# Four-layer graph network on one core: the first layer's scatters add to three DRAM tables in turn instead of four

## The chip, the cores and the metric

The kernel runs on one core of one Trainium2 chip (a core is a set of engines: TensorE, written PE; VectorE, DVE; ScalarE, ACT; GpSimd, POOL; SyncE, SP; with 16 DMA engines beside them). The metric is the device time of one execution in microseconds, as the median over repeated runs; lower is better.

## What is computed

Four message-passing layers run one behind the other on 3125 nodes with 160 features and 100,000 edges. Each layer normalises the nodes, applies a ReLU, builds a message of each edge and adds the messages up by node. The change lies in the first layer, whose reference, cut to what matters, is this:

```python
w = relu(edge_feature @ W_fc1) @ W_fc2            # 224 weights an edge
src, dst = edge_index
xs, xv = s[dst], v[dst]
tp = concatenate([out0a, out0b, out1a, out1b, out1c])   # 480 numbers an edge, from w, xs, xv, edge_attr
agg = segment_sum(tp, src, num_segments=N) / 32.0
out_s = agg[:, :96] @ W_out_s + skip_s
out_v = einsum('nmi,mk->nki', agg[:, 96:].reshape(N, 128, 3), W_out_v) + skip_v
```

The edges are sorted by `dst`. This layer gathers by `dst` and sums by `src`, so its sums go to scattered rows. The other three layers sum by `dst` and keep their sums on the core.

## The kernel before

The edges are padded to 832 tiles of 128 (ALL_TILES), four tiles to a group (GROUP), 208 groups (ALL_GROUPS). The program is written out by hand for each engine and has no planner: each engine's block is a list of instructions in order, and semaphores join the blocks. A barrier of all five engines stands between stages. In the first layer the stages are: the setup, the preparation of the nodes, the edge loop, and the loop behind it (`post`), which works on 25 slots of 128 nodes.

**The setup.** SP loads the inputs and writes zeros over each table `src_sum[c]` (line 420, one DMA of 6240 KB per table). Then it writes the keys (line 425) and comes to the barrier. DVE meanwhile works out the index tables and scales the weights (lines 1361 to 1479).

**The edge loop.** For a group, SP loads the keys (line 474, 256 KB) and the edge features (line 460, 128 KB). PE makes the weights and picks the rows by `dst`, and DVE makes the messages (lines 1574 to 1622 and the many multiplications, which all carry line 1332, that of a helper). In `sums` PE multiplies each tile's 128 messages by a 0/1 matrix (line 1072), so that edges of one tile with the same `src` share one sum. ACT copies each product of 128 x 480 from PSUM to the buffer `E.run` (`run_out`, line 812), which holds two groups. POOL then adds those 128 rows to rows of a table in DRAM (`scatter`, line 628: an indirect DMA with an add, one for each tile, 832 in all). Two such scatters may hit the same row. Those that add to the same table must therefore follow one another: each waits until the last one on its table has landed (semaphore `put[c]`). With CHAINS = 4 tables, tile t of each group goes to table t. ACT waits, before it writes over a piece of `E.run`, until the scatter of two groups earlier that read it has landed.

**The loop behind it.** For each slot SP loads 128 rows of each table (240 KB each, line 511) into `Nv.car`, with two buffers. DVE adds the pieces (`sums`, the lines of 128x480), PE transposes the sum (line 984) and multiplies it by the output weights (lines 1091 and 1093), ACT copies the transposes (lines 850 and 851), and DVE copies the product out (line 1745). On DVE the copy of slot j-2 stands ahead of the additions of slot j; on PE the transposes of slot j stand ahead of the products of slot j-1.

Of the kernel before, what the change touches and what calls it, by code (L numbers as in the profile page):

```python
# [20 lines left out]
ALU = mybir.AluOpType  # L21
# [13 lines left out]
GROUP = 4  # L35
# [5 lines left out]
ALL_TILES = TILES + 2 * MORE  # L41
ALL_GROUPS = ALL_TILES // GROUP
PAD_NODE = ROWS - 1
S, V = 64, 32
CHAINS = 4
DEPTH = 4
ZERO_AT = 18432 - 480

# [53 lines left out]
def build(nc, a, out, layers=(0, 1, 2, 3)):  # L102
    with ExitStack() as ctx:
        def sb(name, shape, dt=F32):
            return ctx.enter_context(nc.sbuf_tensor(name, shape, dt))
# [4 lines left out]
        def dram(name, shape, dt=F32):  # L110
            return nc.dram_tensor(name, shape, dt, kind="Internal").ap()
# [4 lines left out]
        dst_table = dram("dst_table", (ROWS, DIM))  # L116
        src_sum = [dram(f"src_sum{c}", (TABLE_ROWS, SPEC[0]["f"])) for c in range(CHAINS)]
        edge_h = dram("edge_h", (TILES * P, DIM))
# [18 lines left out]
        put_i = sb("put_i", [P, ALL_TILES], I32)  # L137
# [70 lines left out]
        dve_own, act_own, pool_own = sem("dve_own"), sem("act_own"), sem("pool_own")  # L208
# [28 lines left out]
        keys_in = [sem(f"keys_in{b}") for b in range(DEPTH)]  # L237
        put = [sem(f"put{c}") for c in range(CHAINS)]
        s = type("Signals", (), one)
# [52 lines left out]
        def node_views():  # L292
            g = carve()
            v = type("Node", (), {})
            v.h = g(2, DIM)
            v.hT = g(2, 4, P)
            v.big = g(SLOTS * DIM)
            v.small = g(8, SLOTS)
            v.smi = g(SLOTS, dt=I32)
            v.rden = g(SLOTS, 4)  # L300
            v.car = g(2, 4 * 480)
            v.sum = g(2, 480)
            return v

        Nv = node_views()

        def l3_views():
# [90 lines left out]
        def _(sp):  # L398
# [105 lines left out]
            def post():  # L504
                def stage(j, b, first, half):
                    if not first:

                        sp.wait_ge(s.sum_free, 1)
                        sp.sem_inc(s.sum_free, -1)
                    for c in range(CHAINS):  # L510
                        sp.dma_start(Nv.car[:, b, c * 480:(c + 1) * 480],
# [69 lines left out]
        @block.gpsimd  # L581
        def _(pool):
            own = Steps()
            last_row = pool.to_reg(ROWS - 1)
            last_table_row = pool.to_reg(TABLE_ROWS - 1)

            def gather(dst, table, idx, bound):
                return pool.indirect_dma_start(dst, None, table, bass.IndirectOffsetOnAxis(ap=idx, axis=0),  # L588
                                               bounds_check=bound, oob_is_err=True)


            nc.gpsimd.memset(U.zero, 0.0).then_inc(pool_own, own.step())
            nc.gpsimd.memset(ident[:], 0.0).then_inc(pool_own, own.step())
            nc.gpsimd.memset(lower[:], 1.0).then_inc(pool_own, own.step())
            nc.gpsimd.iota(U.columnI, pattern=[[1, P]], base=0, channel_multiplier=0).then_inc(pool_own, own.step())
            nc.gpsimd.iota(U.trashI, pattern=[[0, 2]], base=ROWS, channel_multiplier=1).then_inc(pool_own, own.step())
            pool.wait_ge(pool_own, own.n)
            nc.gpsimd.affine_select(out=ident[:], in_=ident[:], compare_op=ALU.not_equal, fill=1.0, base=0,
                                        pattern=[[-1, P]], channel_multiplier=1).then_inc(pool_own, own.step())

            nc.gpsimd.affine_select(out=lower[:], in_=lower[:], compare_op=ALU.is_gt, fill=0.0, base=0,
                                        pattern=[[-1, P]], channel_multiplier=1).then_inc(pool_own, own.step())
            pool.wait_ge(pool_own, own.n)
            pool.sem_inc(pool_own, own.reset())
            pool.sem_inc(zero_made, 2)

            barrier(pool, "pool")

            def gathers_by_src(l):
                def stage(g):  # L610
                    if g >= DEPTH:

                        pool.wait_ge(s.messages_done, (l - 1) * ALL_GROUPS + g - DEPTH + 1)
                    for t in range(GROUP):
                        e = g * GROUP + t
                        gather(W.got[:, g % DEPTH, t, :], node_table[l], src_i[:, e:e + 1], last_row).then_inc(
                            got[l][g % DEPTH], 16)
                return stage

            def scatter(g):  # L620
                for t in range(GROUP):
                    e = g * GROUP + t

                    if g:
                        pool.wait_ge(put[t], g * 16)

                    pool.wait_ge(s.run_out, e + 1)
                    pool.indirect_dma_start(  # L628
                        src_sum[t], bass.IndirectOffsetOnAxis(ap=put_i[:, e:e + 1], axis=0),
                        E.run[:, g % 2, t * 480:(t + 1) * 480], None, compute_op=ALU.add,  # L630
                        bounds_check=last_table_row, oob_is_err=True).then_inc(put[t], 16)

            barrier(pool, "pool")

            pool.wait_ge(zeroed, 16 * CHAINS)
            unrolled(ALL_GROUPS, [(0, scatter)])
            barrier(pool, "pool")
            barrier(pool, "pool")
            for l in (1, 2):
                nc.gpsimd.memset(acc_view(l), 0.0).then_inc(s.acc_zeroed, 1)  # L640
                barrier(pool, "pool")
                unrolled(ALL_GROUPS, [(0, gathers_by_src(l))])
                barrier(pool, "pool")
                barrier(pool, "pool")
            if 3 in layers:
                barrier(pool, "pool")

                def gather_both(g):
                    b = g % DEPTH
                    if g >= DEPTH:  # L650

                        pool.wait_ge(s.rows_added, g - DEPTH + 1)
                    for t in range(GROUP):
                        e = g * GROUP + t
                        gather(T.gs[:, b, t, :], src_table, src_i[:, e:e + 1], last_row).then_inc(
                            got[3][b], 16)
                        gather(T.gd[:, b, t, :], dst_table, dst_i[:, e:e + 1], last_row).then_inc(
                            got[3][b], 16)
                unrolled(GROUPS, [(0, gather_both)])
                barrier(pool, "pool")  # L660
                barrier(pool, "pool")
                nc.gpsimd.memset(acc_view(3), 0.0).then_inc(s.acc_zeroed, 1)
                barrier(pool, "pool")
                barrier(pool, "pool")
# [13 lines left out]
        def _(act):  # L678
# [17 lines left out]
            for name, key in (("fc2_1", "L1_gnn_fcW2"), ("fc2_2", "L2_gnn_Wfc2"), ("rbf", "L3_gnn_W_rbf")):  # L696
                for to, at, n in BY_Y0:
                    n = min(n, wt[name].shape[1] - to)
# [104 lines left out]
            def run_out(g):  # L803
                b, f = g % 2, SPEC[0]["f"]
                for t in range(GROUP):
                    n = g * GROUP + t
                    if g >= 2:

                        act.wait_ge(put[t], (g - 1) * 16)

                    act.wait_ge(s.run_mm, n + 1)
                    act.activation(E.run[:, b, t * f:(t + 1) * f], bank[:, 6 + n % 2, 0:f], ACT.Copy).then_inc(s.run_out, 1)  # L812
# [78 lines left out]
            prep(0)  # L891
            barrier(act, "act")
            unrolled(ALL_GROUPS, [(0, run_out), (-2, fc_out), (-3, relu_out)])
            for t in range(GROUP):
                act.wait_ge(put[t], ALL_GROUPS * 16)
            barrier(act, "act")
            post()
            barrier(act, "act")
# [428 lines left out]
        def _(dve):  # L1327
            V_ = nc.vector
            c = Steps()

            def tt(o, p, q, op):
                return V_.tensor_tensor(o, p, q, op)  # L1332
# [388 lines left out]
            def post(l):  # L1721
# [3 lines left out]
                def sums(j, b, first, half):  # L1725
                    f = SPEC[0]["f"]

                    dve.wait_ge(s.carry_in0 if b == 0 else s.carry_in1, 16 * CHAINS)
                    dve.sem_inc(s.carry_in0 if b == 0 else s.carry_in1, -(16 * CHAINS))
                    car = Nv.car[:, b, :]  # L1730
                    o = Nv.sum[:, b, 0:f]
                    tt(o, car[:, 0:f], car[:, f:2 * f], ALU.add).then_inc(dve_own, c.step())
                    tt(car[:, 2 * f:3 * f], car[:, 2 * f:3 * f], car[:, 3 * f:4 * f], ALU.add).then_inc(dve_own, c.step())
                    dve.wait_ge(dve_own, c.n)
                    tt(o, o, car[:, 2 * f:3 * f], ALU.add).then_inc(dve_own, c.step())
                    dve.wait_ge(dve_own, c.n)
                    dve.sem_inc(dve_own, c.reset())
                    dve.sem_inc(s.sum_ready, 1)
                    dve.sem_inc(s.sum_free, 1)
# [452 lines left out]
```

## Time and profile before

| what | us |
|---|---|
| median of 3 runs | 8548.7 (8541.74 to 8609.48) |
| the profiled execution's own time | 8655.61 |
| its span | 8653.9 |
| in it: setup and preparation, up to the first edge work | about 205 |
| the edge loop of the first layer | about 205 to 1954 |
| the loop over 25 slots behind it | about 1954 to 2100 |
| layers two to four | the rest |

The profile is of one execution. Starts and durations in it are in microseconds from the span's start. "Busy" is the time in which an engine executes. An idle time is given with what ended it. The granted clock is TensorE's, as a share of full speed. The share of DMA is the mean busy share of the 16 DMA engines, in which a packet counts for the whole of its time, and two that overlap count twice, so that it can pass 1.

### The profile page before, as it was taken

To read this page: it belongs to the slowest core of one execution; us is meant where nothing else is said; L and a number is where in the kernel's file an instruction comes from. 1 tells how busy PE (TensorE), PEld (TensorE's weight loads), DVE (VectorE), ACT (ScalarE), POOL (GpSimd) and SP (SyncE) were. 2 spreads that over 40 slices of the span, in tenths; PEclk is the share of its full clock that TensorE was granted. 3 is DMA by queue.
4 is the path that set the end of the run, shared out by engine and by line. 5 is a ranking of instruction groups with operands and counts; after the bars stand their busy time and mean duration, and the time that the engine had idled before them with its cause. 6 is when DMAs were issued, how large, how long until landed. Compare 5 with 4: busy or idle time off the path is not lost. (4 is left out here: it accounts for less than half of the span.)

```text
span 8653.9 us, 111370 instructions
## 1 busy us (share of the span) xinstructions
PE 7204.2 (83%) x32226; PEld 4840.7 (56%) x32226; DVE 6840.9 (79%) x20357; ACT 3363.3 (39%) x8451; POOL 4980.2 (58%) x4078
## 2 busy tenths in 40 slices
PE   3999999993899999699999947788888888886567
PEld 1444444443455455445544537677777777775455
DVE  5999999994677777577777748778887878787895
ACT  1444444441333233323332325455555555554000
POOL 0777777770566666267766517667767667662000
PEclk9999999995799999689999958888998988898796
DMA  4999999993122222022222112222222222221342
GB/s 163 162 165 169 168 166 168 167 156 117 54 56 57 55 57 56 24 57 61 60 58 59 51 33 67 71 72 75 77 77 72 75 74 75 73 71 47 107 140 80
DMA packets 459615, 776.94 MB, mean 90 GB/s; under 512 B 96641, under 2 KB 310886, under 8 KB 458758
## 3 DMA queue, kind: packets, MB, share of 16 engines
q0 software_dynamic: 274944, 469.50, 28.0%
q1 hardware_dynamic: 178166, 299.52, 11.0%
q8 instruction: 269, 4.41, 0.2%
q14 instruction: 332, 2.72, 0.1%
q10 hardware_dynamic: 5904, 0.79, 0.1%
HBM read 464.60 MB, written 304.85 MB: 89 GB/s over the span
## 5 line engine op out<-in xcount | busy, mean ns | idle before, releaser
L588 POOL DMA_INDIRECT fore<-node_table,src_i x1664 | 1766.6, 1062 | 961.2 <-issue 494.8
L1332 DVE TENSOR_TENSOR work<-work 128x384 f32<-128x384 f32 (+4 forms) x4726 | 1784.7, 406 | 198.5 <-ACT work L922 91.4
L628 POOL DMA_INDIRECT src_sum<-work,put_i x832 | 1323.6, 1591 | 621.8 <-ACT work L812 455.5
L1146 PE MATMUL bank<-work 128*128 128x384 f32 (+1 forms) x3328 | 1359.7, 557 | 94.0 <-DVE work L1332 72.6
L588 POOL DMA_INDIRECT fore<-src_table,src_i x784 | 924.7, 1179 | 820.2 <-DVE work L1332 407.0
L1332 DVE TENSOR_TENSOR work<-work,y 128x384 f32<-128x384 f32 (+2 forms) x2548 | 970.6, 431 | 374.5 <-ACT work L934 248.0
L1146 PEld LDWEIGHTS bank<-work 128*128 128x128 f32 x3328 | 674.5, 213 | 859.5 <-issue 416.0
L588 POOL DMA_INDIRECT fore<-dst_table,dst_i x784 | 943.8, 1204 | 238.9 <-issue 238.9
L1332 DVE TENSOR_TENSOR work<-work,bank 128x384 f32 (+6 forms) x2080 | 896.8, 431 | 154.9 <-remote 73.6
L824 ACT ACTIVATE work<-bank 64x512 f32<-64x512 f32 x416 | 246.0, 591 | 1801.1 <-PE bank L1113 1101.0
L1072 PE MATMUL bank<-work 128*128 128x480 f32 x1664 | 782.1, 605 | 3.1 <-DVE work L1332 2.9
L1127 PE MATMUL bank<-w_fc,work 64*128 64x192 f32 x3328 | 671.8, 343 | 87.5 <-issue 58.4
L1219 PE MATMUL bank<-ident,work 128*128 128x128 f32 x4704 | 697.0, 286 | 52.9 <-DVE work L1332 27.8
L1127 PEld LDWEIGHTS bank<-w_fc,work 64*128 64x128 f32 x3328 | 546.4, 192 | 343.3 <-issue 304.8
L1219 PEld LDWEIGHTS bank<-ident,work 128*128 128x128 f32 x4704 | 552.6, 147 | 169.7 <-issue 127.9
L1332 DVE TENSOR_TENSOR work<-bank,work 128x256 f32<-128x256 f32 x832 | 402.9, 484 | 247.2 <-issue 172.4
L1332 DVE TENSOR_TENSOR work<-bank,aux 128x128 f32<-128x128 f32 (+1 forms) x1248 | 597.0, 479 | 0.0
L812 ACT ACTIVATE work<-bank 128x480 f32<-128x480 f32 x832 | 475.1, 571 | 304.3 <-PE bank L1072 204.3
L840 ACT ACTIVATE work<-fore,y 128x160 f32<-128x160 f32 x1664 | 570.4, 416 | 0.0
L1072 PEld LDWEIGHTS bank<-work 128*128 128x128 f32 x1664 | 272.8, 192 | 520.5 <-issue 278.4
L1237 PE MATMUL bank<-w_val_s,work 96*128 96x164 f32 x1568 | 416.0, 351 | 165.7 <-ACT work L913 103.4
L1332 DVE TENSOR_TENSOR work<-in_window,column 128x512 f32<-128x512 f32 x624 | 427.1, 684 | 93.6 <-PE bank L1146 42.4
(240 smaller groups left out, 12777.6 us busy)
## 6 DMA issues: line engine op xcount, KB each, us to landing
edge_h<-work SPq DMA_DIRECT2D x196, 320.0 KB
work<-edge_h SPq DMA_DIRECT2D x196, 320.0 KB, 2.8
work<-keys SPq DMA_DIRECT2D x196, 256.0 KB
fore<-node_table,src_i POOLq DMA_INDIRECT x1664
work<-in_edge_attr SPq DMA_DIRECT2D x196, 128.0 KB
src_sum<-work SPq DMA_DIRECT2D x4, 6240.0 KB, 41.1
work<-src_sum SPq DMA_DIRECT2D x100, 240.0 KB, 3.3
src_sum<-work,put_i POOLq DMA_INDIRECT x832
```

The source lines that it names most:

```text
L588: return pool.indirect_dma_start(dst, None, table, bass.IndirectOffsetOnAxis(ap=idx, axis=0), bounds_check=bound, oob_is_err=True)
L628: pool.indirect_dma_start(src_sum[t], bass.IndirectOffsetOnAxis(ap=put_i[:, e:e + 1], axis=0), E.run[:, g % 2, t * 480:(t + 1) * 480], Non ...
L812: act.activation(E.run[:, b, t * f:(t + 1) * f], bank[:, 6 + n % 2, 0:f], ACT.Copy).then_inc(s.run_out, 1)
L824: act.activation(W.hid[0:64, b, :], bank[0:64, 0, :], ACT.Silu, scale=(8 ** -0.5, 0.25)[l - 1]).then_inc(s.hidden_out, 1)
L840: last = act.activation(W.by_y0[:, b, t, :], W.got[:, g % DEPTH, t, :], ACT.Copy, scale=y[:, e:e + 1, 0])
L1072: nc.tensor.matmul(bank[:, 6 + n % 2, 0:f], E.sel[:, b, t, :], E.msg[:, b, t * f:(t + 1) * f], start=True, stop=True).then_inc(s.run_mm, 1)
L1127: last = nc.tensor.matmul(wmm(b)[:, t, 0:192], W.hid[0:64, b, t * P:(t + 1) * P], wt[f"fc2_{l}"][:], start=True, stop=True)
L1146: last = nc.tensor.matmul(o, W.sel[:, b, t, :], W.msg[:, b, t * f:(t + 1) * f], start=t == 2 * i, stop=t == 2 * i + 1)
L1219: last = nc.tensor.transpose(bank[:, to + t, i * P:(i + 1) * P], f[:, b, at + t, c0:c0 + P], ident[:])
L1237: nc.tensor.matmul(o[:, 0:164], t1[0:96, t, 0:128], wt["val_s"][:], start=True, stop=True)
L1332: return V_.tensor_tensor(o, p, q, op)
```

## The change

CHAINS becomes 3. Tile e now adds to table e % 3, and waits for the landing of tile e-3 instead of e-4. ACT still waits for the landing of the same scatter as before (that of tile n-8), now counted on that tile's table. SP zeroes three tables, and loads three pieces a slot. DVE adds three pieces with two additions instead of four with three.

```diff
-CHAINS = 4
+CHAINS = 3
...
-            v.car = g(2, 4 * 480)
+            v.car = g(2, CHAINS * 480)
...
-                    if g:
-                        pool.wait_ge(put[t], g * 16)
+                    if e >= CHAINS:
+
+                        pool.wait_ge(put[e % CHAINS], e // CHAINS * 16)
 
                     pool.wait_ge(s.run_out, e + 1)
                     pool.indirect_dma_start(
-                        src_sum[t], bass.IndirectOffsetOnAxis(ap=put_i[:, e:e + 1], axis=0),
+                        src_sum[e % CHAINS], bass.IndirectOffsetOnAxis(ap=put_i[:, e:e + 1], axis=0),
                         E.run[:, g % 2, t * 480:(t + 1) * 480], None, compute_op=ALU.add,
-                        bounds_check=last_table_row, oob_is_err=True).then_inc(put[t], 16)
+                        bounds_check=last_table_row, oob_is_err=True).then_inc(put[e % CHAINS], 16)
...
-                        act.wait_ge(put[t], (g - 1) * 16)
+                        act.wait_ge(put[(n - 2 * GROUP) % CHAINS], ((n - 2 * GROUP) // CHAINS + 1) * 16)
...
-            for t in range(GROUP):
-                act.wait_ge(put[t], ALL_GROUPS * 16)
+            for k in range(CHAINS):
+                act.wait_ge(put[k], (ALL_TILES + CHAINS - 1 - k) // CHAINS * 16)
...
                     tt(o, car[:, 0:f], car[:, f:2 * f], ALU.add).then_inc(dve_own, c.step())
-                    tt(car[:, 2 * f:3 * f], car[:, 2 * f:3 * f], car[:, 3 * f:4 * f], ALU.add).then_inc(dve_own, c.step())
                     dve.wait_ge(dve_own, c.n)
                     tt(o, o, car[:, 2 * f:3 * f], ALU.add).then_inc(dve_own, c.step())
```

On POOL, at the start of the edge loop, the kernel before reads so. A row is one instruction, with what it waits for; put0 to put3 are the semaphores of the four tables, and run_out is ACT's copy.

```order
14 L628 DMA src_sum<-work,put_i 3328x480 [waits pool_own,phase,run_out,zeroed]
15 L628 DMA src_sum<-work,put_i 3328x480 [waits run_out] x3
16 L628 DMA src_sum<-work,put_i 3328x480 [waits run_out,put0]
17 L628 DMA src_sum<-work,put_i 3328x480 [waits run_out,put1]
18 L628 DMA src_sum<-work,put_i 3328x480 [waits run_out,put2]
19 L628 DMA src_sum<-work,put_i 3328x480 [waits run_out,put3]
20 L628 DMA src_sum<-work,put_i 3328x480 [waits run_out,put0]
```

The changed kernel's POOL, at the same place:

```order
14 L629 DMA src_sum<-work,put_i 3328x480 [waits pool_own,phase,run_out,zeroed]
15 L629 DMA src_sum<-work,put_i 3328x480 [waits run_out] x2
16 L629 DMA src_sum<-work,put_i 3328x480 [waits run_out,put0]
17 L629 DMA src_sum<-work,put_i 3328x480 [waits run_out,put1]
18 L629 DMA src_sum<-work,put_i 3328x480 [waits run_out,put2]
19 L629 DMA src_sum<-work,put_i 3328x480 [waits run_out,put0]
20 L629 DMA src_sum<-work,put_i 3328x480 [waits run_out,put1]
```

No scatter is added, removed or moved. The fourth already waits for the first, and each later one waits for the third before it.

On DVE, at the start of the loop over the slots, the kernel before reads so (carry_in0 and carry_in1 are the loads of a slot's pieces; L1332 is the line of the helper for additions):

```order
4964 L1332 TENSOR_TENSOR work<-work 128x480 [waits dve_own,phase,carry_in0]
4965 L1332 TENSOR_TENSOR work<-work 128x480
4966 L1332 TENSOR_TENSOR work<-work 128x480 [waits dve_own]
4967 L1332 TENSOR_TENSOR work<-work 128x480 [waits dve_own,carry_in1]
4968 L1332 TENSOR_TENSOR work<-work 128x480
4969 L1332 TENSOR_TENSOR work<-work 128x480 [waits dve_own]
4970 L1745 COPY fore<-bank 128x192 [waits dve_own,node_mm]
```

The changed kernel's DVE, at the same place (the helper now stands on line 1333):

```order
4964 L1333 TENSOR_TENSOR work<-work 128x480 [waits dve_own,phase,carry_in0]
4965 L1333 TENSOR_TENSOR work<-work 128x480 [waits dve_own]
4966 L1333 TENSOR_TENSOR work<-work 128x480 [waits dve_own,carry_in1]
4967 L1333 TENSOR_TENSOR work<-work 128x480 [waits dve_own]
4968 L1745 COPY fore<-bank 128x192 [waits dve_own,node_mm]
```

The addition that waited for nothing is gone, 25 times; what is left waits as before.

## Rows read from the trace of the kernel before

**Rows 1.** Busy time by stretch (windows from:to, length, engines, clock, DMA share, GB/s).

```profile
205.00:1937.00 1732.00, 1649.54 (x5395) 823.06 (x5396) 1691.17 (x6856) 821.76 (x1451) 1314.27 (x826) 0.99 0.96 164
1954.00:2097.00 143.00, 61.92 (x284) 59.15 (x285) 55.44 (x98) 15.74 (x48) 0.00 (x0) 0.50 0.55 172
```

**Rows 2.** Waits in the edge loop (total us, times, longest) of DVE and POOL.

```profile
DVE work L1574 <- PE bank L1060: 36.9, 40, 7.7
...
POOL src_sum L628 <- ACT work L812: 455.5, 333, 220.4
...
POOL src_sum L628 <- DMA src_sum<-work,put_i: 8.7, 21, 0.7
```

**Rows 3.** Timeline of POOL in the edge loop (start, duration, idle before and its end).

```profile
223.18 1.76 POOL L628 DMA_INDIRECT src_sum<-work,put_i  x1 [220.40 <-ACT work L812]
...
766.05 1.55 POOL L628 DMA_INDIRECT src_sum<-work,put_i  x1 [0.31 <-issue]
767.91 1.55 POOL L628 DMA_INDIRECT src_sum<-work,put_i  x1 [0.30 <-issue]
...
773.89 1.60 POOL L628 DMA_INDIRECT src_sum<-work,put_i  x1 [0.73 <-DMA src_sum<-work,put_i]
...
1946.58 1.55 POOL L628 DMA_INDIRECT src_sum<-work,put_i  x1 [0.30 <-issue]
```

**Rows 4.** Timeline of SP: the loads beside the scatters at 766 us.

```profile
768.30 0.33 SPq L474 DMA_DIRECT2D work<-keys  x1
768.68 0.50 SPq L460 DMA_DIRECT2D work<-in_edge_attr  x1
```

**Rows 5.** Busy time in short stretches: the first scatter's data, and the last's.

```profile
225.00:225.50 0.50, 0.50 (x3) 0.22 (x3) 0.00 (x0) 0.06 (x2) 0.25 (x1) 1.00 0.00 0
225.50:226.00 0.50, 0.50 (x5) 0.50 (x5) 0.00 (x0) 0.50 (x1) 0.50 (x1) 1.00 1.40 88
...
1950.00:1951.00 1.00, 0.00 (x0) 0.00 (x0) 0.00 (x0) 0.00 (x0) 0.00 (x0) 0.50 0.87 154
1951.00:1952.00 1.00, 0.00 (x0) 0.00 (x0) 0.00 (x0) 0.00 (x0) 0.00 (x0) 0.50 0.04 6
```

**Rows 6.** DMA queues, 1000 to 1200 us (packets, MB, share of 16 engines).

```profile
q0 software_dynamic: 13837, 23.62, 80.0%
q1 hardware_dynamic: 5376, 9.44, 17.3%
```

**Rows 7.** Timeline of one slot of the loop behind, all engines.

```profile
1973.68 0.36 DVE L1745 COPY fore<-bank 128x192 f32<-128x192 f32 x1 [3.06 <-DVEq L1744]
1974.39 1.92 DVE L1332 TENSOR_TENSOR work<-work 128x480 f32<-128x480 f32 x3 [0.35 <-DVEq L1729]
1976.61 1.06 PE L984 MATMUL bank<-ident,work 128*96 128x128 f32 x4 [3.08 <-PEq L1079]
1976.65 1.74 SPq L511 DMA_DIRECT2D work<-src_sum  x4
...
1977.84 1.38 PE L1093 MATMUL bank<-w_out_v,work 128*128 128x32 f32 x6
1979.37 0.36 DVE L1745 COPY fore<-bank 128x192 f32<-128x192 f32 x1 [3.06 <-DVEq L1744]
```

**Rows 8.** DVE's additions from 1954 to 2100 us (busy, mean ns, idle before).

```profile
L1332 DVE TENSOR_TENSOR work<-work 128x480 f32<-128x480 f32 x75 | 47.2, 657 | 33.4 <-DVEq L1729 32.5
```

**Rows 9.** Timeline of the setup: SP's last zero fill and key writes, DVE's last work.

```profile
50.13 16.38 SPq L420 DMA_DIRECT2D src_sum<-work  x1
66.55 20.51 SPq L425 DMA_DIRECT2D keys<-work  x2
...
115.82 0.29 DVE L1479 TENSOR_SCALAR w_lin_x<-w_lin_x,w 128x128 f32<-128x128 f32 x1
```

**Rows 10.** Busy time in the setup, before and behind the end of its DMAs.

```profile
10.00:92.00 82.00, 0.50 (x2) 0.39 (x2) 39.20 (x74) 3.62 (x4) 0.00 (x0) 1.00 1.06 378
92.00:113.00 21.00, 0.00 (x0) 0.00 (x0) 18.16 (x134) 0.00 (x0) 0.00 (x0) 1.00 0.00 1
```

## The prediction

> **What bounds the kernel now.** I read the busy time by stretch first, to find the engine that sets each of the two loops that the change touches. In the edge loop, of the 1732 us from 205 to 1937, DVE is busy for 1691 (98%), and its waits on PE come to 37 us [rows 1, 2]. PE is busy for 1650 (95%), POOL for 1314. DVE is the bound. But the DMA engines stand at 0.96 of their time [rows 1], and the scatters are what fills them: in 200 us the POOL queue took 80.0% and the loads of SP 17.3% [rows 6]. So the question is whether the scatters, each now waiting for the third before it, can keep up with DVE.
>
> The pace they must keep: from the first scatter's start at 223.18 to the last's at 1946.58 there are 831 steps [rows 3], 2.074 us each, or 8.30 us a group of four. POOL itself needs 1.55 us and an idle 0.30, so 1.86 a scatter and 7.42 a group [rows 3]; 0.88 us a group is slack. That is why the waits of POOL read as they do: mostly for ACT's copy, and only 21 times in 832, 8.7 us in all, for a landing [rows 2].
>
> In the loop behind, from 1954 to 2097, no engine is busy half the time, DMA stands at 0.55, and the clock granted is 0.50 [rows 1], the lower of TensorE's two levels, 1.2 GHz; PE had been idle while the last scatters drained. The timeline of a slot shows a ring: DVE copies a product out (0.36), idles 0.35, makes three additions (1.92), then PE transposes (1.06) and multiplies (to the end of the 1.38 us group of line 1093), and only then can DVE copy again. From copy to copy it is 1979.37 - 1973.68 = 5.69 us [rows 7].
>
> **The loop behind, part by part.** One addition of 128x480 goes from each of 25 slots. They last 657 ns each on average, 75 of them [rows 8], and three take 1.92 us together [rows 7], so the next one begins some 0.03 us before the last one's end, and one is worth 0.62 to 0.66 us. It stands in the ring, ahead of the transposes, so nothing hides it and it is gained in full: 25 x 0.62 = 15.5 us. What is late next is the same ring, at 5.69 - 0.62 = 5.07 us. The quarter less of loads is hidden: SP issues the four loads of a slot in 1.74 us right behind the additions that freed their buffer [rows 7], and their pieces are not added until two slots later, over 9 us on. Only before the first slot does anything wait for them: one piece less, 240 KB, is at most 1.4 us at the 172 GB/s of this stretch [rows 1]; I take 0.5. Bounds for this part: nothing gained if the ring had another limit that takes over, and 25 x 5.69 / 4 = 36 us gained if, against the rows, the loads set the pace and it fell with their number. I take -16.
>
> **The setup.** One zero fill of four goes; the last took SP 16.38 us, and the key writes behind it end at 87 us [rows 9]. The DMA engines are done by about 92 us, yet DVE works on for another 24 us, up to 116 [rows 9, 10], and the barrier needs DVE. So a fill is worth nothing while DVE covers it; if it were not covered it would be worth up to 16 us. I take 0.
>
> **The edge loop.** Nothing is added: the same 832 scatters, in the same order, with one wait each. Only the distance of the wait shrinks. How long does a landing take, from the start of a scatter? The trace bounds it. With nothing else under way, the first scatter's start is at 223.18, and its data first shows after 225.5 [rows 3, 5]; the last one's start is at 1946.58 and the data ends at about 1951.05 [rows 3, 5]: 4.5 us. That is the lower end. At the upper, the scatter at 773.89 was released by a landing, that of the fourth before it, which began at 766.05 [rows 3]: 7.84, less the 0.30 that POOL idles anyway, is 7.5 us. SP's 384 KB of keys and features were issued at 768.30 and 768.68 [rows 4], and shared the engines with it. Since four scatters take 7.42 us or more, and POOL waited for a landing in 2.5% of the cases, nearly all landings take under 7.5. Between 4.5 and 7.5 I take the middle, 6.0.
>
> With three tables at most three scatters are under way, so a group of four needs 4/3 of a landing and of the 0.1 us that I allow for the release (an estimate; the rows don't show it apart). At 6.0 that is 8.13 us, under the 8.30 that DVE needs. Break-even is a mean landing of 8.30 x 3/4 - 0.1 = 6.1 us. So the loop comes out just unhurt, with a margin of 0.1 us, and each further 0.1 us would cost 0.13 x 208 = 28 us. At the lower end, 4.5, the loop costs nothing; at the upper, 7.5 for each, 10.1 us a group, 1.8 x 208 = +380 us. I lean to the good side of the margin for two reasons. With fewer scatters ahead of it in the queue, a landing should be sooner, not later. And a late scatter isn't yet a late group: `E.run` holds two groups, so ACT needs the landing of a group's last scatter 2 x 8.30 = 16.6 us after its copy, while that scatter starts 5.6 us behind the group's first and lands 7.5 us later at worst, at 13.1. POOL can thus be 3.5 us behind before ACT, and behind it PE (its bank), then DVE, waits. But scatters vary, and not every loss is made up: I charge 10 us, about a third of a tenth over the margin, which also covers a later end of the last scatters.
>
> The Trainium skill, page "DMA: Bandwidth & Descriptors", section "Anatomy of one DMA — SWDGE (gpsimd) path", gives a fit for such a DMA, 2.0 us and its bytes by 436 GB/s. By that the 240 KB would take 2.6 us behind the issue of 1.55, 4.1 in all, three tables would do with much to spare, and the sum would be -16 alone, 8533. The trace doesn't agree inside the loop: 4.5 with nothing else under way, up to 7.5 beside the loads.
>
> **The sum.** -16 for the loop behind, 0 for the setup, +10 for the edge loop: -6. Against the profiled execution's own 8655.6 that gives 8650. That execution was 107 us above the median of the runs, 8548.7; the difference carries over, so I forecast 8548.7 - 6 = 8543. A measurement of this kernel can tell a change of about 1%, 85 us, from none, so this one would not be seen as a change.
>
> **Rival A, slower: one slow landing in each group.** The mean is not all that counts. SP's loads come once a group, and the scatter that shares the engines with them lands late. If each group has one that takes 7.0 us (between my 6.0 and the 7.5 seen), the third behind it waits for that, and the one behind this needs POOL's 1.86: a ring of 7.0 + 0.1 + 1.86 = 8.96 us a group against 8.30. That costs 0.66 x 208 = 137, less 16: +121, 8670. It decides as soon as that one landing takes more than 8.30 - 1.96 = 6.3 us. For it: the 7.5 beside loads, and DMA engines at 0.96, where any gap is lost for good. Against it: POOL falls behind the loads as it slips, so the slow scatter moves, or shares its delay with its neighbour, and the ring opens. The same page of the Trainium skill, section "SWDGE vs HWDGE vs iDMA", says that each DMA engine goes round robin between the two kinds of queue, which is what such a slow scatter would come from. Chance 0.13.
>
> **Rival B: more is gained.** With a shorter ring, PE is busy a larger share of it; should the clock go back to 2.4 GHz, its 3.0 us or so a slot would halve: 25 x 1.5 = 38 more, with a loop that costs nothing -54, 8495. Against it: 62 us busy of 143 now [rows 1] would be 62 of 127, 49%, hardly other. Should the zero fill lie on the path after all, 16 more. Chance 0.06.
>
> **Rival C: the change is hidden.** The loads or SP's issue keep the slot's pace at 5.69, so that nothing is gained there, and the edge loop pays 10 to 40 us: 8559 to 8589. For it: little, SP's issue is 1.74 us of 5.69. Chance 0.11.
>
> **How the numbers follow.** The forecast has 0.70: the slot at 5.07 us and the edge loop within 0 to +30, so 8533 to 8563, and with the scatter of the runs some 20 us to either side. All but rival A lie within 1%. A mean landing a little above break-even would reach up to it. For slower by over 1% I give 0.13, faster 0.03 (nothing in the rows is worth 85 us), same 0.84. The range takes in rival B's larger part, rival C and the near side of A: 8505 to 8655.
>
> **What would show it.** DVE's additions x50 in the loop behind and 5.07 us from copy to copy; that loop some 16 us shorter. In the edge loop, POOL's idle time before a scatter goes from ACT's copy to the landing, in hundreds of cases instead of 21, with DVE still 98% busy and 8.30 to 8.35 us a group. It is wrong if DVE shows waits on PE, PE on ACT and ACT on the landing, and a group takes over 8.7 us; or if the first edge work begins 10 us or more earlier, which would put the zero fill on the path.

## The result: slower by 1.5%

The changed kernel takes 8710.7 us as a median of 4 runs (8699.5 to 8719.7), the kernel before 8567.0 beside it (4 runs). The ratio on record is 1.0153, with an interval of 1.0119 to 1.0188: by that it is 131 us slower, somewhere between 102 and 161 (the two medians by themselves differ by 144). The forecast was 8543, in a range from 8505 to 8655. It was wrong, and the case that came true is by its size rival A, at 8670.

The pages of the two kernels show where POOL's time went. These are their rows for the scatters, before and changed: busy time, mean ns, idle time before them, and what ended most of it.

```profile
L628 POOL DMA_INDIRECT src_sum<-work,put_i x832 | 1323.6, 1591 | 621.8 <-ACT work L812 455.5
```

```profile
L629 POOL DMA_INDIRECT src_sum<-work,put_i x832 | 1314.1, 1579 | 762.6 <-DMA src_sum<-work,put_i 349.2
```

Busy and idle time together, less the 220.5 us before the first scatter, are 1856.2 us in the changed kernel, or 8.92 a group of four. The kernel before has 1725.0 in the same way, or 8.29. This loop loses 0.63 x 208 = 131 us. That the ratio gives 131 as well is chance: the loop behind gains 14 (below), so the parts give 117, which lies inside the interval.

The waits in the same stretch, from 205 to 2100 us (total, times, longest), answer to [rows 2]:

```profile
POOL src_sum L629 <- DMA src_sum<-work,put_i: 349.2, 236, 3.1
POOL src_sum L629 <- ACT work L813: 283.0, 169, 220.5
ACT work L813 <- DMA src_sum<-work,put_i: 177.5, 120, 4.1
...
DVE work L1575 <- PE bank L1061: 139.0, 74, 7.8
```

POOL waits for a landing 236 times where it was 21. The waits are passed on: ACT waits for a landing up to 4.1 us (at most 0.7 before), because the buffer of two groups earlier is not free, and DVE waits 139 us for PE where it was 37. The busy times by stretch (clock, DMA share and GB/s at the end, as in [rows 1]):

```profile
205.00:2068.00 1863.00, 1729.94 (x5403) 853.63 (x5402) 1692.51 (x6856) 816.21 (x1454) 1304.78 (x826) 0.95 0.90 153
2085.00:2215.00 130.00, 63.36 (x292) 60.59 (x292) 41.18 (x73) 16.28 (x50) 0.00 (x0) 0.50 0.45 142
76.00:92.00 16.00, 0.00 (x0) 0.00 (x0) 14.62 (x54) 0.00 (x0) 0.00 (x0) 1.00 0.00 1
```

In the edge loop DVE does the same 1691 to 1693 us of work, now in 1863 us instead of 1732, so it is busy for 91% and no longer the bound. The DMA engines went down, from 0.96 to 0.90 and from 164 to 153 GB/s. So they, too, did less per microsecond as the loop got slower. What the loop ran out of is scatters under way; the experiments below test that.

A piece of POOL's timeline shows the pattern, which comes back about once a group:

```profile
1003.62 1.55 POOL L629 DMA_INDIRECT src_sum<-work,put_i  x1 [0.30 <-issue]
1005.47 1.55 POOL L629 DMA_INDIRECT src_sum<-work,put_i  x1 [0.30 <-ACT work L813]
1007.33 1.55 POOL L629 DMA_INDIRECT src_sum<-work,put_i  x1 [0.30 <-ACT work L813]
1010.39 1.57 POOL L629 DMA_INDIRECT src_sum<-work,put_i  x1 [1.51 <-DMA src_sum<-work,put_i]
1012.26 1.55 POOL L629 DMA_INDIRECT src_sum<-work,put_i  x1 [0.30 <-issue]
1014.12 1.55 POOL L629 DMA_INDIRECT src_sum<-work,put_i  x1 [0.30 <-ACT work L813]
1016.38 2.19 POOL L629 DMA_INDIRECT src_sum<-work,put_i  x1 [0.71 <-DMA src_sum<-work,put_i]
```

The scatter at 1010.39 waited for the third before it, which had started at 1003.62; it could not start 1.86 us behind its neighbour, but 3.06. Those behind it then went at POOL's own pace of 1.86, not at the pace of the landings. What a late landing costs is not won back by an early one.

The loop behind went as forecast. Its timeline on DVE:

```profile
2112.66 0.36 DVE L1745 COPY fore<-bank 128x192 f32<-128x192 f32 x1 [3.06 <-DVEq L1744]
2113.37 1.35 DVE L1333 TENSOR_TENSOR work<-work 128x480 f32<-128x480 f32 x2 [0.35 <-DVEq L1730]
2117.79 0.36 DVE L1745 COPY fore<-bank 128x192 f32<-128x192 f32 x1 [3.06 <-DVEq L1744]
```

Two additions take 1.35 us where three took 1.92, and a slot 5.13 us where it took 5.69 [rows 7]. SP's first to last load of the slots, on the kernel before and on the changed one:

```profile
1954.35 132.19 SPq L511 DMA_DIRECT2D work<-src_sum  x100
```

```profile
2085.73 118.01 SPq L511 DMA_DIRECT2D work<-src_sum  x75
```

That is 14 us less. In the setup the DMA engines are now done by 76 us (the stretch from 76 to 92 above has a share of 0.00), and the first scatter still starts at 223 us: the zero fill was covered, as forecast.

### The profile page after: what moved, and what is told of

It is laid out like the page before. It is cut to its first block and busy times, and to the rows that moved or that the text cites. A ratio compares the mean times of both kernels' runs of the same rounds, so it can differ in the third digit from the quotient of the medians.

```text
span 8717.9 us, 111319 instructions
## 1 busy us (share of the span) xinstructions
PE 7287.3 (84%) x32226; PEld 4883.4 (56%) x32226; DVE 6830.6 (78%) x20332; ACT 3355.8 (38%) x8451; POOL 5015.1 (58%) x4078
## 3 DMA queue, kind: packets, MB, share of 16 engines
q10 hardware_dynamic: 5904, 0.79, 0.1%
## 5 line engine op out<-in xcount | busy, mean ns | idle before, releaser
L1333 DVE TENSOR_TENSOR work<-work 128x128 f32<-128x128 f32 (+3 forms) x4701 | 1768.7, 405 | 240.4 <-ACT work L923 165.8
L588 POOL DMA_INDIRECT fore<-src_table,src_i x784 | 949.4, 1211 | 746.9 <-DVE work L1333 317.1
L1147 PEld LDWEIGHTS bank<-work 128*128 128x128 f32 x3328 | 670.9, 212 | 846.9 <-issue 407.9
L588 POOL DMA_INDIRECT fore<-dst_table,dst_i x784 | 969.3, 1236 | 239.0 <-issue 239.0
L1073 PE MATMUL bank<-work 128*128 128x480 f32 x1664 | 834.1, 640 | 3.2 <-DVE work L1333 2.8
L1073 PEld LDWEIGHTS bank<-work 128*128 128x128 f32 x1664 | 296.8, 206 | 566.0 <-issue 327.3
```

The lines of the kernel that those rows point to most:

```text
L1073: nc.tensor.matmul(bank[:, 6 + n % 2, 0:f], E.sel[:, b, t, :], E.msg[:, b, t * f:(t + 1) * f], start=True, stop=True).then_inc(s.run_mm, 1)
L1147: last = nc.tensor.matmul(o, W.sel[:, b, t, :], W.msg[:, b, t * f:(t + 1) * f], start=t == 2 * i, stop=t == 2 * i + 1)
```

## The experiments

The eleven rows of results are from three chips of unlike speed, here called A, B and C (the kernel before takes 8012, 8583 and 8007 us on them), so each kernel is compared with the kernel before on its own chip. The time of a group comes from the page's row for the scatters of each run, as above: busy and idle time, less the wait before the first, over 208. A group of four tables takes 8.3 us on all three chips (8.34, 8.32 and, with five tables, 8.35), so that groups can be compared from chip to chip to some 0.03 us.

| kernel | chip | ratio (95% interval) | group, us |
|---|---|---|---|
| changed, run again | B | 1.0159 (1.0109 to 1.0209) | 9.06 |
| only the loop behind changed | A | 0.9982 (0.9959 to 1.0004) | 8.34 |
| four tables, wait for the third before | A | 1.0177 (1.0139 to 1.0216) | 9.03 |
| three tables, light loads | A | 1.0012 (0.9989 to 1.0035) | 8.41 |
| three tables, three groups of buffers | A | 1.0172 (1.0133 to 1.0212) | 9.04 |
| three tables, keys loaded in two halves | B | 1.0106 (1.0063 to 1.0148) | 8.90 |
| four tables, wait for the second before | C | 1.0798 (1.0760 to 1.0836) | 11.17 |
| four tables, light loads | C | 0.9984 (0.9967 to 1.0002) | 8.25 |
| five tables | C | 1.0012 (0.9997 to 1.0027) | 8.35 |
| four tables, additions first | B | 0.9956 (0.9931 to 0.9981) | 8.32 |
| three tables, additions first | B | 1.0103 (1.0054 to 1.0153) | 9.01 |

The changed kernel, run again, lost what it had lost the first time; 1.5 to 1.7% was expected. Kernels that leave out a table's sums or part of the loads compute something else and serve as measurements alone.

### The loop behind alone

```diff
-                    for c in range(CHAINS):
+                    for c in range(3):
                         sp.dma_start(Nv.car[:, b, c * 480:(c + 1) * 480],
...
-                    tt(car[:, 2 * f:3 * f], car[:, 2 * f:3 * f], car[:, 3 * f:4 * f], ALU.add).then_inc(dve_own, c.step())
```

> The kernel before, with the loop behind the edge loop alone changed: it loads and adds three of the four tables (the fourth table's sums are left out of the output). Theory (the loss is the edge loop's, the gain the slots'): the edge loop stays at 8.30 us a group, a slot goes from 5.69 to about 5.05 us, and the time falls by 16 us, to about 8551 against 8567 for before. Rival (the slots' gain is not real, or PE's low clock moves): no difference, or more than 30 us.

The ratio of 0.9982 is -14 us of 8012, with an interval from -33 to +3, so the time alone doesn't settle it; the trace does. SP's loads of the slots take 117.88 us in this run (118.01 in the changed kernel), and the slot is 5.12 us, against 5.13 there:

```profile
2001.52 0.36 DVE L1744 COPY fore<-bank 128x192 f32<-128x192 f32 x1 [3.06 <-DVEq L1743]
2002.23 1.35 DVE L1332 TENSOR_TENSOR work<-work 128x480 f32<-128x480 f32 x2 [0.35 <-DVEq L1729]
2006.64 0.36 DVE L1744 COPY fore<-bank 128x192 f32<-128x192 f32 x1 [3.06 <-DVEq L1743]
```

### The distance of the wait alone

```diff
-                    if g:
-                        pool.wait_ge(put[t], g * 16)
+                    if e >= 3:
+                        pool.wait_ge(put[(e - 3) % 4], ((e - 3) // 4 + 1) * 16)
+                    if e >= 4:
+                        pool.wait_ge(put[t], g * 16)
```

> The kernel before with four tables, but each scatter also waits for the landing of the third before it, so that at most three are under way. Theory (the distance of the wait is what costs: one slow landing, the release and one more issue make a ring of about 8.9 us a group): the edge loop takes 8.9 us a group as in the changed kernel, and the time is the changed kernel's plus the 16 us that the slots give back, about 8725. Rival (fewer tables make the landings themselves slower, by where the rows lie): 8.30 us a group and about 8567.

The ratio is 1.0177, +142 us, and a group takes 9.03 us. Its waits are those of the changed kernel:

```profile
POOL src_sum L630 <- DMA src_sum<-work,put_i: 375.0, 244, 3.9
```

So the whole loss is in how many scatters may be under way. That there are three tables instead of four, and where their rows lie, costs nothing that can be seen. The two parts add up: 1.0177 less the 0.18% of the slots gives 1.0159, what the changed kernel has on chip B.

### Light loads, with three tables and with four

The keys by dst are not loaded and those by src are used in their place; of the edge features 16 rows of 64 are loaded from the fifth group on. SP's bytes fall from 384 to about 160 KB a group.

```diff
-                    sp.dma_start(E.attr[0:64, b, :], attrs64[:, g * 512:(g + 1) * 512]).then_inc(here, 16)
+                    sp.dma_start(E.attr[0:16, b, :], attrs64[0:16, g * 512:(g + 1) * 512]).then_inc(here, 16)
...
-                    sp.dma_start(E.keys[:, b].rearrange("p t w n -> p (t w n)"),
-                                 keys16.rearrange("(g n) -> g n", n=1024)[g:g + 1, :]
+                    sp.dma_start(E.own[:, b].rearrange("p t n -> p (t n)"),
+                                 own16.rearrange("(g n) -> g n", n=512)[g:g + 1, :]
```

> The changed kernel with SP's loads in the edge loop cut from 384 KB to about 160 KB a group: the keys by dst are not loaded (those by src stand in for them) and only 16 of 64 rows of edge features are. What it leaves out is the gather by dst and most of the edge features. Theory (the scatter that shares the DMA engines with the loads is the slow one that closes the ring): POOL's waits for landings fall from 349 us to under 100, the group goes back to about 8.3 us, and the time falls by some 100 us or more, to about 8600 or below. Rival (three landings are too few at any load, or TensorE's clock is the cause by itself): above 8680.

> The kernel before, with four tables, and SP's loads cut as in the kernel with three tables and light loads (the keys by dst and three quarters of the edge features left out). It says what the light loads give by themselves. Theory (four tables lose nothing to landings, so lighter loads give nothing): the time of the kernel before within 10 us, a group at 8.2 to 8.3 us. Rival (the full DMA engines slow the loop in other ways too, by late keys or features): 30 us or more below it.

With three tables the ratio falls to 1.0012 and a group to 8.41 us; with four tables the same cut gives 0.9984 and 8.25. So light loads give little by themselves, and the price of three tables in the edge loop falls from 0.63 x 208 = 131 us (0.69 x 208 = 144 on chip A) to 0.16 x 208 = 33, from two runs on different chips. The time fell by about 118 us, from the changed kernel's ratio of 1.0159 to 1.0012, where some 100 or more were expected. The loads matter, but the first expectation was wrong in its picture. The waits for landings, which were to fall under 100 us in all, did not become rare. They became short:

```profile
POOL src_sum L635 <- DMA src_sum<-work,put_i: 265.6, 290, 2.6
```

290 waits of 0.9 us each, where the changed kernel had 236 of 1.5. With four tables and light loads there are 12, of 4.5 us in all. By its time that kernel is 13 us under the kernel before (0.9984, interval 0.9967 to 1.0002), between its theory and its rival, and not told apart from none.

### A deeper buffer

```diff
-            v.run = g(2, GROUP * 480)
+            v.run_rows = [*[g(GROUP * 480) for _ in range(2)], work[:, 18432 - GROUP * 480:18432]]
...
-                        act.wait_ge(put[(n - 2 * GROUP) % CHAINS], ((n - 2 * GROUP) // CHAINS + 1) * 16)
+                        act.wait_ge(put[(n - RUNS * GROUP) % CHAINS], ((n - RUNS * GROUP) // CHAINS + 1) * 16)
```

> The changed kernel with three groups of buffers for the summed messages instead of two, so that ACT waits for the landing of twelve tiles earlier instead of eight. Theory (POOL's ring is a limit of throughput, and a buffer only lets it fall further behind before the others feel it): the same time within 10 us, 8700 to 8715. Rival (the ring by itself is fast enough, and the loss comes from uneven landings that the small buffer passes on to ACT and PE): the loop goes back towards 8.3 us a group, below 8640.

The ratio is 1.0172 and a group 9.04 us: nothing gained. That ACT waits for landings is a consequence. POOL with three scatters under way is too slow by itself, and a buffer only lets it fall further behind.

### The burst of loads cut in two

```diff
+            def edge_keys_2(g):
+                if g >= GROUPS:
+                    return
+                if g >= DEPTH:
+                    sp.wait_ge(s.edges_done, g - DEPTH + 1)
+                half_keys(g, 1)
...
-            unrolled(ALL_GROUPS, [(-2, edge_keys), (0, edge_scalars)])
+            unrolled(ALL_GROUPS, [(-2, edge_keys), (0, edge_scalars), (-2, edge_keys_2)])
```

> The changed kernel with the load of a group's keys (256 KB) cut into two halves, the second issued when DVE has ended a group, some 5 us behind the first; all that is loaded is still loaded. Theory (the ring is closed by one slow landing a group, about 6.7 us, made slow by the burst of loads): with the burst cut, the slowest landing is about 0.4 us sooner, a group takes 8.4 to 8.7 us instead of 8.9, and the time is 40 to 100 us below the changed kernel's. Rival (the loads slow the scatters by their bytes, whenever they come, since the DMA engines are full): the same time as the changed kernel within 15 us.

Between the two: 8680 against 8717 us, 36 less, just under what the theory asked for, and the two intervals overlap (1.0063 to 1.0148, and 1.0109 to 1.0209). The trace has 0.16 us a group less, 8.90 for 9.06, which is 33 us. There are more waits for landings than before, 336, and shorter ones. Cutting the burst takes away about a fifth of the loss. It didn't take the late landings away, though: by the completion events in the traces (explained below), 95 in 100 landings take under 7.3 us with the keys in two halves and under 7.5 in the changed kernel on the same chip, and the mean is 6.0 in both. Each half now has late neighbours of its own: 267 scatters start less than 2 us ahead of one and land after 6.6 us on average, where the changed kernel has 195, after 6.8. So this run doesn't refute a ring closed by the late landings; what it shows is that more than one landing a group counts.

### How far the wait reaches: two, and five

```diff
+                    if e >= 2:
+                        pool.wait_ge(put[(e - 2) % 4], ((e - 2) // 4 + 1) * 16)
```

> The kernel before with four tables, but each scatter waits for the landing of the second before it: at most two under way. Theory (a scatter starts 1.86 us behind the one before or 0.26 us behind the landing that it waits for, whichever is later; landings come sooner with less ahead of them): landings fall to about 5.0 us from the scatter's start, nearly every start waits for one, 2 x 5.26 = 10.5 us a group, some 450 us over the kernel before. Rival (a landing takes 6.0 us however many are under way): 12.5 us a group and some 870 us over.

```diff
-CHAINS = 4
+CHAINS = 5
...
-                    for c in range(CHAINS):
+                    for c in range(4):
```

> Five tables, so that each scatter waits for the landing of the fifth before it; the loop behind loads and adds four of them (the fifth table's sums are left out of the output). Theory (with four tables POOL waits for a landing in 2 to 4% of the cases and nobody behind it does): the edge loop and the time as in the kernel before within 10 us. Rival (the step from three to four goes on from four to five, uneven landings still cost something): 20 us or more below it.

With two under way the ratio is 1.0798, 639 us over, and a group takes 11.17 us: more than the 450 us and the 10.5 expected, less than the rival's 870 and 12.5. The landings were sooner (5.25 us on average, below), and the group is again longer than their mean gives, 2 x (5.25 + 0.27) = 11.0. Five tables change nothing that can be told from none: 1.0012 (0.9997 to 1.0027) and 8.35 us. Its POOL no longer shows a wait for a landing at all, only these:

```profile
POOL src_sum L629 <- ACT work L813: 469.8, 325, 220.6
POOL src_sum L629 <- issue: 167.5, 507, 2.6
```

So the curve is 11.17, 9.03, 8.3, 8.35 for two, three, four and five under way. With four, DVE sets the pace and the landings are hidden behind it; with three they set it.

### The additions first

```diff
-            v.sum = g(2, 480)
+            v.sum = g(3, 480)
...
-                    pipelined(dve, SLOTS, [(2, products), (0, sums)])
+                    pipelined(dve, SLOTS, [(0, sums), (2, products)])
```

> The kernel before with one thing changed in the loop behind: DVE adds the pieces of slot j before it copies out the product of slot j-2, with three buffers for the sums instead of two. Theory (a slot is a ring of DVE's additions, PE's transposes and products and DVE's copy): the ring opens, since the additions no longer wait for PE, and a slot falls from 5.7 to about 4 us, so the time is some 40 us (0.5%) below the kernel before. Rival (the loads of four pieces set the pace as soon as the ring is open, at 960 KB and some 300 GB/s, 3.3 us, or PE does): no more than 20 us.

> The changed kernel with the same new order of DVE's work in the loop behind. Theory: a slot takes what PE takes, 3 to 4 us, with three pieces as with four, so the time is 30 to 40 us below the changed kernel's and the gain of the third table in the slots is gone. Rival (DVE's additions still count): a slot is 0.6 us shorter than with four tables.

With four tables the ratio is 0.9956 (0.9931 to 0.9981), 38 us under the kernel before (16 to 59): the lowest ratio of all here. The ring of [rows 7], in which DVE's additions wait for a product that PE has not made yet, is open: 100 loads now take 97.55 us instead of 132.19, and additions follow additions after 3.8 us.

```profile
2028.13 1.92 DVE L1332 TENSOR_TENSOR work<-work 128x480 f32<-128x480 f32 x3 [1.25 <-DVEq L1729]
2030.50 0.36 DVE L1745 COPY fore<-bank 128x192 f32<-128x192 f32 x1 [0.45 <-DVEq L1744]
2031.91 1.92 DVE L1332 TENSOR_TENSOR work<-work 128x480 f32<-128x480 f32 x3 [1.05 <-DVEq L1729]
```

With three tables the same order gives 78.92 us for the loads, against 118.01. Here the theory was wrong and its rival nearer: with the ring open the gain of one table less is not gone, it is 97.6 - 78.9 = 19 us where it was 14. The addition taken out is 0.57 x 25 = 14 of them. The other 5 may be the loads, which run at 250 GB/s and a DMA share of 0.81 with four pieces; that isn't shown. The gain is still far less than the edge loop's loss: 1.0103.

## Why the prediction was wrong, and where it was right

**The loop behind** was right in mechanism and size: a term of -16 measured -14. The removed addition was worth 0.57 us and not 0.62: 1.92 - 1.35.

**The setup** was right: a fourth zero fill covered by DVE's work, worth 0.

**The edge loop** is where it failed, at the step "so a group of four needs 4/3 of a landing and of the 0.1 us that I allow for the release". The numbers put into it were nearly right. The traces record the completion events of each table's semaphore (no view lists them one by one), and from these come the landings, counted from a scatter's start. The mean is 5.9 us with four tables and 5.9 with three, where I had taken 6.0. In these two traces 15 and 8% of the events are missing, but two traces of chip A have them all and say the same: 6.1 us with four under way, 6.0 with three. The release is 0.27 us and not 0.1. By the forecast's rule that makes 8.2 to 8.4 us a group. Measured were 8.92 and, on chip A, 9.03.

What the rule leaves out is that a scatter starts at the later of two times: 1.86 us behind its neighbour, or 0.27 us behind the landing of the third before it. Landings spread, from 4.5 us (5 in 100 are under it) to 7.3 (95 in 100 are) in the changed kernel. A late one delays POOL; an early one gives nothing, for POOL can't go faster than 1.86. So what counts is the mean of the later of the two, not the later of the two means. A calculation tests that rule: landings drawn at random from those of a run, each start by the rule. It gives 8.96 us a group for the changed kernel (measured 8.92), 9.1 for four tables with three under way (9.03), 8.42 with light loads (8.41; landings of 5.7 on average, 4.8 to 6.8), 9.03 with split keys (8.90), and 11.3 with two under way (11.17; landings of 5.25). For four under way it gives 7.5, below DVE's 8.3, so there POOL isn't the bound. The 1.86 and 0.27 are read from the timelines, none is fitted, and no case is off by more than 0.2 us. In the run with light loads DVE's own pace (8.25) is so near that part of the agreement may be luck.

Each of these takes the landings of the very run that it explains. The stronger test takes those of the kernel before and asks what three under way would make of them: 8.9 us a group, drawn at random or in their own order, against 8.92 measured; and from the trace of chip A with four under way, 9.0 to 9.2 against 9.03. So the trace of the kernel before held the loss already. For two under way it doesn't work (12.6 to 13.2 for 11.17), since there the landings themselves become sooner.

**The reading of the shortest landing** was a little off as well: "with nothing else under way" isn't so for the last scatter, which had others ahead of it, and the end of its data at 1951.05 is not its landing, which the events put 5.2 us after its start. The first scatter, which had nothing ahead of it, landed 4.8 to 5.0 us after its start in eight of the nine traces that have all its events (5.9 in the one with split keys).

**The two reasons for leaning to the good side** both failed. "A landing should be sooner, not later", with fewer ahead: at three under way the mean was the same as at four; only at two was it sooner, 5.25. And "POOL can be 3.5 us behind before ACT waits" is a loan, not a pace. A loop that loses 0.6 us a group has used it up after six groups; the three groups of buffers showed that a bigger loan changes nothing.

**Rival A** had the right size, 8.96 us, and more of the cause than it was given. Its late landing is there in the events: with four under way (chip A, all events) the fourth scatter of a group lands after 7.0 us on average, the other three after 5.6 to 5.9. With the measured release its ring is 7.0 + 0.27 + 1.86 = 9.1 us, as near to the 9.03 as the calculation above, so the time of a group alone doesn't tell the two apart. The argument against it was that the slow scatter would move as POOL slips against the loads. It does move, but it doesn't go away: with three under way 107 of the 832 scatters still start less than 1 us ahead of a load of keys and land after 7.1 us on average, and 106 start 1 to 2 us ahead and land after 6.2. The order of the program explains it (an argument, no run takes it apart): the loads are issued as DVE gets on, DVE follows POOL, and so the loads keep step with the scatters that they slow. What rival A lacks is that other landings count too, as the 336 waits with split keys and the 290 with light loads show. Its chance of 0.13 was too small: a margin of 0.1 us on a mean, with landings known to reach 7.5, was no margin.

**TensorE's clock** is a thing that the prediction didn't speak of for this loop. The granted clock was 0.99 there and is now 0.95. Is that a cause? Two stretches of the changed kernel and one of the kernel before, all with the clock at 1.00 throughout:

```profile
1557.00:1621.00 64.00, 58.33 (x197) 29.45 (x196) 60.45 (x245) 29.34 (x53) 44.35 (x29) 1.00 0.92 157
1932.00:2034.00 102.00, 92.83 (x310) 46.50 (x309) 94.62 (x388) 46.91 (x83) 73.47 (x46) 1.00 0.93 157
```

```profile
952.50:1105.50 153.00, 146.20 (x489) 73.21 (x487) 149.74 (x611) 73.59 (x130) 118.18 (x76) 1.00 0.98 168
```

From the scatters' starts a group takes 9.18 and 8.84 us in the first two and 8.22 in the third (the counts behind "x" take in scatters cut by a window's edge). Short windows vary, so here is the whole loop: at full clock, 1642 us of it, a group takes 8.99 us in the changed kernel, and in the one before 8.23, over 1685 us. The loss is there without the clock's fall. At the lower level the changed kernel spends 211 us, in 41 stretches of at most 7 us, and a group takes 8.5 us in them. So the time was not lost there, since POOL sets the pace.

**What doesn't add up to the last.** With two under way the loop explains (11.17 - 8.34) x 208 = 589 of the 639 us that the ratio gives. Of the profiled executions on chip C, that one also took 65 us longer than the one with five tables in layers two to four, which neither touches (5970 against 5904 us; the one with four tables and light loads took 5967). And the profiled executions of the kernel before and the changed one differ by only 64 us in span, since in the former layers two to four, which the change doesn't touch, took 53 us longer. Why these layers vary by that much is open.

## What to carry to other kernels

When a wait lets at most k transfers be under way, don't compare k times the pace with the mean landing. Each start is the later of two times, so take the landings of the kernel that you have, with their spread and in their order, and run them through that rule with the new k: here it gives 8.9 us a group, where the mean gave 8.2 and DVE needed 8.3. It holds as long as the landings stay as they are, which they did from four to three and not from four to two. A deeper buffer behind the late engine doesn't help against a pace that is too slow. When the late engine becomes the bound, whatever is triggered by the others' progress may keep step with it and stay in its way. And look for the ring before counting instructions in it: by the traces, reordering two stages on DVE was worth 35 us, and an addition taken out 14.

## What the runs showed of the hardware

A scatter with an add of 128 rows of 1920 bytes kept POOL for 1.55 us, and the next could start 0.30 us behind. It landed 4.8 to 5.0 us after its start with nothing of its kind ahead of it (5.9 in one trace of nine). Inside the loop, with the DMA engines at 0.90 to 0.98, it landed after 6.0 to 6.1 us on average, and 95 in 100 landed within 7.4 (chip A). Those that started less than 1 us ahead of a load of 384 KB landed after 7.1 us on average. Going from four under way to three left the mean where it was, and going to two took 0.8 us off it. The DMA engines' busy share fell with the number under way, from 0.96 to 0.90 with three and to 0.80 with two, and the loop got slower each time: a high share was no sign that fewer would do. The next scatter started 0.27 us behind the landing that it waited for, in every kernel in which scatters waited often.
